# Cross-attention slots in 64 x 64 quarters, with the attended rows copied out of PSUM by VectorE

## The chip, the cores and the metric

The kernel runs on one core of one Trainium2 chip. The metric is the device time of one launch in microseconds (us), of which the median of several runs is taken. TensorE (PE) multiplies, VectorE (DVE), ScalarE (ACT) and GpSimd (POOL) compute element by element, and SyncE (SP) starts most transfers. PEld is TensorE's stream of weight loads.

## The reference

A decoder layer on 16 sequences of 128 tokens with 256 features, in three residual stages: self-attention in emulated fixed point, cross-attention on a context of 128 rows with 128 features, and a feed-forward net with a low-rank part for each of two experts. Only the cross-attention is changed:

```python
qh = (q @ Wq).reshape(B, N, NUM_HEADS, HEAD_DIM).transpose(0, 2, 1, 3)   # 16 heads of 64
kh = (kv @ Wk).reshape(B, M, NUM_HEADS, HEAD_DIM).transpose(0, 2, 1, 3)
vh = (kv @ Wv).reshape(B, M, NUM_HEADS, HEAD_DIM).transpose(0, 2, 1, 3)
attn = jax.nn.softmax(jnp.einsum('bhnd,bhmd->bhnm', qh, kh) * scale, axis=-1)
out = jnp.einsum('bhnm,bhmd->bhnd', attn, vh)
return out.transpose(0, 2, 1, 3).reshape(B, N, INNER) @ Wo + bo
```

## The kernel before

The 16 sequences go in 4 groups (g) of 4, so 512 tokens. The self-attention stage comes first, then the cross-attention stage, then the feed-forward stage. A cross group has 8 **slots** (s), one for each pair of heads. With n = 8 g + s, slot n computes the query, key and value blocks of its pair and its scores, while the softmax, the transposes and the attends lag behind: in slot s TensorE transposes and attends pair n - 3 (`LAG = 3`) and projects pair n - 4. Groups 0 and 1 are written out as straight code and groups 2 and 3 are one loop (`Fori`, L870 for TensorE). Group 1 also merges a low-rank product into feed-forward weights in its slots 3 to 6 (`b_merge`, L783). After the last group come drain slots that finish the lagging work beside the first feed-forward blocks.

TensorE runs its slot in a fixed order, `b_slot` (L792): transposes (L751), q block, v block, projection, k block, attends (L764), scores (L776). Slot 0 splits the projection around transposes, q and v; slot 7 puts the transposes of the next group's normed rows (`normed_T`, L582) between attends and scores. q, k, v and projection go through `split3` (L561 to L566): three products of rounded high and low parts, with full 128 x 128 weights. Attends and scores multiply plain 32-bit floats; an attend has 128 rows (keys) and 64 columns of the array (a head), a score has 64 rows (a head) and 128 columns. The two heads of a pair sit side by side, in the column halves for attends, in the row halves for scores.

PSUM has 8 banks of 128 x 512 floats (L149 to L156): the projection sums in 0 and 1, q and k share bank 2 (`one_ps`), v and the first half of the transposes share bank 3, scores have 4 and 5, the other half of the transposes 6, and the attended rows 7 (`o_ps`).

VectorE's slot (L1392): two reductions of the scores (`neg_max`, L1399), two copies of the transposed weights (`aT_sb`, L1412), the v copy (L1373), parts of the next group's normalisation, the k copy (L1390), the reciprocal (L1445), and the low part of the attended rows (`oT_lo`, L1454). ScalarE's slot (L1062): the q copy (L1096), eight exponentials (L1074), and the high part of the attended rows (`oT_hi`, L1116), read from bank 7. GpSimd scales the exponentials (`b_weights`, L441). Every hand-over is a counting semaphore: `b_S` counts score halves, `b_av` attends, `b_olo` the `oT_lo` that the projection waits for, and so on.

## Time and profile before

| | us |
|---|---|
| median of 3 runs | 642.77 (642.34 to 642.79) |
| the profiled execution | 642.12 |
| its span, first to last instruction | 640.3 |

| engine | busy us | share of the span |
|---|---|---|
| PE | 633.0 | 99% |
| PEld | 548.3 | 86% |
| DVE | 501.2 | 78% |
| ACT | 414.9 | 65% |
| POOL | 346.8 | 54% |

The cross slots run from about 276 us to 522 us of the span. In a row of the timeline stand start, length, engine, line, operation, output and inputs, shape and count; records of one line that follow each other are merged, and the length then goes from the first start to the last end. Each 32-bit product is two records. The end of a matmul record is modelled and lies behind the start of the next one, so rates are read from the distance of starts.

### The profile page before, as it was taken

What the parts mean: (1) busy time and instruction counts of PE and PEld (TensorE: products, weight loads), DVE (VectorE), ACT (ScalarE), POOL (GpSimd) and SP (SyncE); (2) the same over time, 40 slices, a digit from 0 to 9 for tenths busy, and PEclk for the clock granted to TensorE, in tenths of its full rate; (3) what the DMA queues carried; (4) which work ended last, traced back from release to release, by engine and by line L of the source; (5) the groups of instructions that cost most, each with busy time, mean ns of one, the idle gap of its engine ahead of it and who ended that gap; (6) DMA issues with size and microseconds to landing.
All of it is one profiled execution on the core that took longest, in us unless ns stands there. A gap on an engine that the chain in (4) does not pass through costs nothing.

```text
span 640.3 us, 16035 instructions
## 1 busy us (share of the span) xinstructions
PE 633.0 (99%) x5333; PEld 548.3 (86%) x5333; DVE 501.2 (78%) x975; ACT 414.9 (65%) x1458; POOL 346.8 (54%) x742
## 2 busy tenths in 40 slices
PE   8999999999999999999999999999999999999998
PEld 5788888888888888888888888888888888888987
DVE  6888799978998899877777777666667659878765
ACT  4788788888888888887555666565645554434432
POOL 4898376756666666865587675565366433010100
DMA  7954000000000000031100000000000000010010
GB/s 217 383 211 178 1 2 2 2 1 0 0 0 0 0 1 0 16 133 67 48 2 18 1 3 3 16 2 3 1 0 0 0 1 2 1 34 21 12 34 33
DMA packets 10005, 23.14 MB, mean 36 GB/s; under 512 B 1618, under 2 KB 6018, under 8 KB 9058
## 3 DMA queue, kind: packets, MB, share of 16 engines
q1 hardware_dynamic: 7794, 14.63, 6.6%
q0 software_dynamic: 1440, 7.08, 3.1%
q10 hardware_dynamic: 720, 0.79, 0.3%
q8 instruction: 27, 0.44, 0.3%
q14 instruction: 24, 0.20, 0.1%
HBM read 20.40 MB, written 2.10 MB: 35 GB/s over the span
## 4 chain that ended last, share of the span: by engine, by line
PE 92%; POOL 3%; DVE 2%; issue 1%; ACT 1%; DMA 0%; SPq 0%; DVEq 0%; POOLq 0%; ACTq 0%
PE bank L564 21%; PE bank L566 20%; PE bank L565 20%; PE bank L776 5%; PE bank L764 5%; PE bank L751 5%; PE bank L629 5%; PE bank L652 5%; PE bank L618 3%; PE bank L582 2%; PE bank L897 1%; POOL p_int L349 1%; DVE hid L1500 0%; DMA x_sb<-in_x 0%; POOL wv_lo L310 0%
## 5 line engine op out<-in xcount | busy, mean ns | idle before, releaser
L441 POOL TENSOR_SCALAR p_f<-e_sb,rsum 128x128 f32<-128x128 f32 x256 | 90.2, 374 | 83.8 <-DVE rsum L1445 83.4
L349 POOL TENSOR_SCALAR p_int<-e_sb,rsc 128x128 int16<-128x128 f32 x256 | 106.6, 435 | 6.3 <-issue 5.9
L1074 ACT ACTIVATE e_sb<-bank,neg_max 128x128 f32<-128x128 f32 x256 | 90.1, 385 | 4.7 <-DVE neg_max L1399 4.6
L970 ACT ACTIVATE sgn<-bank 128x512 bf16<-128x512 f32 x96 | 54.4, 605 | 33.9 <-PE bank L566 33.9
L985 ACT ACTIVATE e_sb<-si 128x128 f32<-128x128 int16 x256 | 76.1, 314 | 0.2 <-DVE si L1252 0.2
L1230 DVE SCALAR_TENSOR_TENSOR ri<-sgn,bank 128x512 int16<-128x512 bf16 x96 | 63.3, 684 | 12.1 <-ACT sgn L970 10.8
L1096 ACT ACTIVATE q_sb<-bank 128x512 f32<-128x512 f32 x32 | 19.2, 600 | 70.4 <-PE bank L566 70.4
L1074 ACT ACTIVATION_READ_ACCUMULATOR e_sb<-bank,neg_max 128x1 f32 x256 | 57.5, 225 | 0.0
L564 PE MATMUL bank<-xnT_hi,wqk_lo 128*128 128x512 f32 x128 | 53.1, 414 | 1.1 <-DVE ri L1230 0.7
L985 ACT ACTIVATION_READ_ACCUMULATOR e_sb<-si 128x1 f32 x256 | 52.5, 205 | 0.0
L566 PE MATMUL bank<-xnT_hi,wqk_hi 128*128 128x512 f32 x128 | 50.2, 392 | 0.0
L565 PE MATMUL bank<-xnT_lo,wqk_hi 128*128 128x512 f32 x128 | 50.1, 391 | 0.0
L344 POOL TENSOR_TENSOR rsc<-rsum,growth 128x8 f32<-128x8 f32 x32 | 7.4, 232 | 69.8 <-DVE rsum L1286 69.8
L1390 DVE COPY k_sb<-bank 128x512 f32<-128x512 f32 x32 | 22.1, 692 | 27.8 <-PE bank L566 27.7
L1157 ACT CAST oT_hi<-hid 128x512 fp32r<-128x512 f32 x32 | 19.9, 621 | 36.4 <-DVE hid L1500 36.4
L1454 DVE TENSOR_TENSOR oT_lo<-bank,oT_hi 128x512 fp32r<-128x512 f32 x32 | 22.1, 692 | 26.2 <-ACT oT_hi L1116 26.2
L1399 DVE TENSOR_REDUCE neg_max<-bank 128x4 f32<-128x512 f32 x64 | 40.9, 682 | 0.0
L1346 DVE SCALAR_TENSOR_TENSOR si<-s_sgn,bank 128x512 int16<-128x512 bf16 x64 | 40.9, 679 | 0.0
L1412 DVE COPY aT_sb<-bank 128x512 f32<-128x512 f32 x63 | 40.4, 682 | 0.2 <-PE bank L751 0.2
L336 POOL TENSOR_SCALAR veps<-mv 128x4 f32<-128x4 f32 x12 | 3.3, 274 | 64.0 <-DVE mv L1197 63.9
L564 PE MATMUL bank<-wv_hi,xnT_lo 128*128 128x256 f32 x128 | 37.3, 292 | 0.2
L564 PE MATMUL bank<-cw_hi,oT_lo 128*128 128x256 f32 x128 | 36.8, 288 | 0.6 <-DVE oT_lo L1492 0.3
(159 smaller groups left out, 2149.5 us busy)
## 6 DMA issues: line engine op xcount, KB each, us to landing
wB_raw<-in_wB SPq DMA_DIRECT2D x1, 3072.0 KB, 17.6
wB_hi<-in_wB POOLq DMA_DIRECT2D x1, 3072.0 KB, 11.1
wqk_raw<-in_wqk SPq DMA_DIRECT2D x8, 256.0 KB, 8.5
x_sb<-in_x SPq DMA_DIRECT2D x3, 512.0 KB, 16.2
out<-x_sb SPq DMA_DIRECT2D x6, 256.0 KB, 2.2
wqk_hi<-in_wqk POOLq DMA_DIRECT2D x5, 256.0 KB, 7.2
wp_raw<-in_wp SPq DMA_DIRECT2D x1, 1024.0 KB, 13.1
wp_hi<-in_wp POOLq DMA_DIRECT2D x1, 1024.0 KB, 9.1
```

Of the source, the lines that this page charges most:

```text
L349: i = nc.gpsimd.tensor_scalar(p_int[:, half, t, :], e_sb[:, half, t, :], rsc[:, half, t:t + 1], -0.5, ALU.mult, ALU.add)
L441: i = nc.gpsimd.tensor_scalar(p_f[:, half, t, :], e_sb[:, half, t, :], rsum[:, half, t:t + 1], 0.0, ALU.mult, ALU.add)
L564: pe.matmul(out_, wl, mh, start=first, stop=False, **kw)
L565: pe.matmul(out_, wh, ml, start=False, stop=False, **kw)
L566: return pe.matmul(out_, wh, mh, start=False, stop=last, **kw)
L970: nc.scalar.activation(sgn[:, m % 2, :], proj_ps[m % 2][:, :], ACT.Sign).then_inc(a_sgn, 1)
L985: last = nc.scalar.activation(e_sb[:, half, t, :], si[:, i, j * P:(j + 1) * P], ACT.Exp, scale=1.0 / FIX, accum_out=sums[:, t:t + 1])
L1074: last = nc.scalar.activation(e_sb[:, (s - 1) % 2, t, :], s_ps[hh][:, (t % 4) * P:(t % 4 + 1) * P], ACT.Exp, bias=neg_max[:, t:t + 1], sca ...
L1230: V.scalar_tensor_tensor(ri[:, m % 2, :], sgn[:, m % 2, :], -0.5, proj_ps[m % 2][:, :], ALU.mult, ALU.add).then_inc(a_ri, 1)
L1346: V.scalar_tensor_tensor(si[:, i, :], s_sgn[:, i, :], -0.5, s_ps[i][:, :], ALU.mult, ALU.add).then_inc(a_si, 1)
L1399: V.tensor_reduce(neg_max[:, half], s_ps[hh][:, :].rearrange("p (a t) -> p a t", a=GB), AX, ALU.min).then_inc(b_mx, 1)
L1412: V.tensor_copy(aT_sb[:, GB * hh:GB * hh + GB, :].rearrange("p a t -> p (a t)"), pT_ps[hh][:, :]).then_inc((b_pT0, b_pT)[hh], 1)
```

## The change

In the slots from slot 3 of group 0 on (`opens_b` is true for the three before it):

- Scores and attends are issued as 64 x 64 quarters (`b_scores_quarters`, `b_attend_quarters`). Scores: each head's queries are split in two halves. Attends: the keys are split in two halves; the first step takes keys half 0 for two sequences and half 1 for the other two, the second step the opposite, and each adds to one of two banks (`o_pair`).
- TensorE's order becomes transposes, q, k, v, (merge), projection, (next group's transposes), attends step 0, scores, attends step 1.
- Banks: `o_pair` takes half of bank 6 and half of bank 7, which are also k's and q's; v and the two halves of the transposes take 2 and 3.
- VectorE copies the attended rows to a new SBUF tile, `o_raw`, between its two score reductions of the next slot. q waits for that copy (`b_raw`). ScalarE makes `oT_hi` from `o_raw`, and VectorE `oT_lo`, now behind the `aT_sb` copies of the next slot.
- ScalarE does the first four exponentials before the q copy in all slots. VectorE copies k before v. The context's high and low parts for the next group are made in slot 7 in place of slot 0. The loops over groups 2 and 3 are written out for PE, ACT and DVE.
- In the first drain slot the second half of the transposes waits for `b_raw`, and the projection is no longer split.

```diff
--- before.py
+++ after.py
...
+    o_raw, _, nxt = place("o_raw", [P, TOK], F32, at=nxt)
...
-    banks = [nc.alloc_psum_tensor(f"bank{i}", [P, 512], F32) for i in range(8)]
+    banks = [nc.alloc_psum_tensor(f"bank{i}", [P, 512], F32) for i in range(6)]
+    pair = nc.alloc_psum_tensor("pair", [P, 1024], F32)
+    banks += [pair[:, 0:512], pair[:, 512:1024]]
+    o_pair = pair[:, :].rearrange("p (a f) -> p a f", a=2)[:, :, 0:TOK // 2]
     y_ps = banks[0:2]
     proj_ps = banks[2:4]
     s_ps = banks[4:6]
     t_ps = banks[6]
     o_ps = banks[7]
-    one_ps, v_ps = banks[2], banks[3]
-    pT_ps = (banks[3], banks[6])
+    q_ps, k_ps, v_ps = banks[7], banks[6], banks[2]
+    pT_ps = (banks[2], banks[3])
+    first_qk_ps, first_v_ps = banks[2], banks[3]
+    drain_pT_ps = (banks[3], banks[6])
     low_ps = banks[2]
...
             def b_block(g, s, what):
-
+                n = NP * g + s
                 if what == "q":
+                    out_ = first_qk_ps if opens_b(g, s) else q_ps
                     wait(pe, ln_lo, 2 * (G + g) + 2)
-                    wait(pe, b_k, NP * g + s)
+                    if opens_b(g, s):
+                        wait(pe, b_k, n)
+                    else:
+                        wait(pe, b_raw, n - LAG)
+                        if n == LAG:
+                            pe.wait_ge(a_oi, NP * G)
                     for kt in range(KD):
-                        last = split3(one_ps[:, :], [w[kt][:, s * P:(s + 1) * P] for w in (wq_hi, wq_lo)],
+                        last = split3(out_[:, :], [w[kt][:, s * P:(s + 1) * P] for w in (wq_hi, wq_lo)],
                                       [t[:, kt, :] for t in (xnT_hi, xnT_lo)], kt == 0, kt == KD - 1)
...
-                    last = split3(one_ps[:, :], [w[:, s * P:(s + 1) * P] for w in (wk_hi, wk_lo)],
+                    out_ = first_qk_ps if opens_b(g, s) else k_ps
+                    if opens_b(g, s):
+                        wait(pe, b_q, n + 1)
+                    elif n == LAG:
+                        pe.wait_ge(a_aT, NP * G)
+                    if s == 0:
+                        wait(pe, b_clo, g + 1)
+                    last = split3(out_[:, :], [w[:, s * P:(s + 1) * P] for w in (wk_hi, wk_lo)],
...
-                    wait(pe, b_pT0, NP * g + s - LAG + 1)
+                    out_ = first_v_ps if opens_b(g, s) else v_ps
+                    wait(pe, b_pT0, n - LAG + 1)
...
                 last.then_inc(b_blk, 1)
 
-            def b_transpose(n, half, summed=0):
+            def b_transpose(g, s, drain, merging):
+                n = NP * g + s - LAG
+                half = n % 2
                 wait(pe, b_p, n + 1)
-                if isinstance(n, int) and n == 0:
-                    wait(pe, a_aT, NP * G)
-                wait(pe, b_pT, n)
+                if s > 0 and not drain:
+                    wait(pe, b_v, NP * g + s)
+                if n == 0:
+                    pe.wait_ge(b_k, LAG)
                 for hh in range(2):
-                    if hh == 1 and summed:
-                        pe.wait_ge(m_sum, summed)
+                    out_ = (drain_pT_ps if drain else pT_ps)[hh]
+                    if s == 0:
+                        wait(pe, ln_lo, 2 * (G + g) + (2 if drain else hh + 1))
+                    if hh == 0:
+                        wait(pe, b_pT0, n)
+                    else:
+                        wait(pe, b_pT, n)
+                        if drain and s == 0:
+                            wait(pe, b_raw, n)
+                        if merging and s > 3:
+                            pe.wait_ge(m_sum, s - 3)
                     for b in range(GB):
-                        last = pe.transpose(pT_ps[hh][:, b * P:(b + 1) * P], p_f[:, half, GB * hh + b, :], ident[:, :])
+                        last = pe.transpose(out_[:, b * P:(b + 1) * P], p_f[:, half, GB * hh + b, :], ident[:, :])
                 last.then_inc(b_T, 1)
+
+            def b_attend_quarters(n, p, v_count, step):
+
+                if step == 0:
+                    wait(pe, b_pT, n + 1)
+                    wait(pe, b_v, v_count)
+                    wait(pe, b_q, n + LAG + 1)
+                    wait(pe, b_k, n + LAG + 1)
+                else:
+                    wait(pe, b_half, n + 1)
+                for b in range(2):
+                    for keys in range(2):
+                        side = keys ^ step
+                        for hh in range(2):
+                            h0 = (2 * p + hh) * DH
+                            at = slice(keys * DH, (keys + 1) * DH)
+                            last = pe.matmul(o_pair[hh * DH:(hh + 1) * DH, side, b * P:(b + 1) * P],
+                                             v_sb[at, 2 * side + b, h0:h0 + DH], aT_sb[at, GB * hh + 2 * side + b, :],
+                                             start=step == 0 and b == 0, stop=step == 1, skip_group_check=True)
+                last.then_inc((b_half, b_av)[step], 1)
+
+            def b_scores_quarters(n, s):
+                wait(pe, b_q, n + 1)
+                wait(pe, b_k, n + 1)
+                wait(pe, b_e, n)
+                for b in range(GB):
+                    for rows in range(2):
+                        for hh in range(2):
+                            at = b * P + rows * DH
+                            last = pe.matmul(s_ps[hh][rows * DH:(rows + 1) * DH, b * P:(b + 1) * P],
+                                             q_sb[hh * DH:(hh + 1) * DH, s % 2, at:at + DH],
+                                             k_sb[hh * DH:(hh + 1) * DH, s % 2, b * P:(b + 1) * P],
+                                             start=True, stop=True)
+                            if b == GB - 1 and rows == 1:
+                                last.then_inc(b_S, 1)
...
-                    wait(pe, a_oi, NP * G)
+                wait(pe, b_raw, NP * G - LAG)
...
                 if drain:
-                    if s == 0:
-                        project((0, 1))
                     transposes()
                     if s == 0:
                         c_low(0, True)
-                        project((2, 3))
-                    else:
-                        if s < LAG:
-                            c_up(0, s - 1)
-                        project()
+                    elif s < LAG:
+                        c_up(0, s - 1)
+                    project()
...
+                if opens_b(g, s):
...
+                    attend()
+                    b_scores(g, n, s)
+                    return
+                transposes()
+                b_block(g, s, "q")
+                b_block(g, s, "k")
+                b_block(g, s, "v")
+                if merging and s in (3, 4, 5, 6):
+                    wait(pe, b_pT, n - LAG + 1)
+                    b_merge(s - 3)
+                project()
                 if s == NP - 1:
                     def free():
-                        wait(pe, b_k, n + 1)
                         wait(pe, b_v, n + 1)
+                        wait(pe, b_pT, n - LAG + 1)
                     normed_T(G + g + 1, free)
-                b_scores(g, n, s)
+                p = (s - LAG) % NP
+                gg = g if s >= LAG else g - 1
+                v_count = NP * gg + 2 * (p // 2) + 2
+                b_attend_quarters(n - LAG, p, v_count, 0)
+                b_scores_quarters(n, s)
+                b_attend_quarters(n - LAG, p, v_count, 1)
...
-                if first and s == LAG:
-                    act.wait_ge(b_T, 1)
-                    wait(act, a_av, NP * G)
...
                     if first and s < 2:
                         wait(act, a_S, 2 * (NP * G + s) - 2)
-                    nc.scalar.activation(q_sb[:, s % 2, :], one_ps[:, :], ACT.Copy, scale=-DH ** -0.5).then_inc(b_q, 1)
...
+                        act.wait_ge(ld_ctx, 16 * (g + 2))
+                        act.wait_ge(b_blk, BLOCKS * (g + 1))
+                        nc.scalar.copy(cT_hi[:, :], cT_raw[:, :]).then_inc(b_chi, 1)
+                    xnT_high(G + g + 1)
...
-                    nc.scalar.copy(oT_hi[:, :], o_ps[:, :]).then_inc(b_ohi, 1)
-                if s == LAG and not first and not drain:
...
+                        wait(act, b_pj, n - LAG)
+                        nc.scalar.copy(oT_hi[:, :], o_ps[:, :]).then_inc(b_ohi, 1)
+                    else:
+                        wait(act, b_pj, n - LAG)
+                        wait(act, b_raw, n - LAG + 1)
+                        nc.scalar.copy(oT_hi[:, :], o_raw[:, :]).then_inc(b_ohi, 1)
 
             for s in range(NP):
                 b_slot(0, s, first=True)
...
                 n = NP * g + s
@@ -1395,33 +1467,43 @@
                 if (not (first and s == 0)) and not (drain and s >= 1):
                     for hh in range(2):
                         wait(dve, b_S, 2 * n - 1 + hh)
+                        if hh == 1 and n > LAG:
+                            wait(dve, b_av, n - LAG)
+                            wait(dve, b_olo, n - LAG - 1)
+                            V.tensor_copy(o_raw[:, :].rearrange("p (a f) -> p a f", a=2), o_pair).then_inc(b_raw, 1)
                         half = slice(GB * hh, GB * hh + GB)
                         V.tensor_reduce(neg_max[:, half], s_ps[hh][:, :].rearrange("p (a t) -> p a t", a=GB), AX,
...
                     a_out_low(NP * G + s - 1 - LAG)
+                if drain and s == 0:
+                    low_rows(n - LAG - 1, o_raw)
                 if lagged:
                     wait(dve, b_T, n - LAG + 1)
                     if first and s == LAG:
                         wait(dve, a_av, NP * G)
                     wait(dve, b_av, n - LAG)
-                    for hh in range(1 if first and s == LAG else 0, 2):
+                    for hh in range(2):
                         V.tensor_copy(aT_sb[:, GB * hh:GB * hh + GB, :].rearrange("p a t -> p (a t)"),
-                                      pT_ps[hh][:, :]).then_inc((b_pT0, b_pT)[hh], 1)
+                                      (drain_pT_ps if drain else pT_ps)[hh][:, :]).then_inc((b_pT0, b_pT)[hh], 1)
+                if first and s == LAG:
...
+                if opens_b(g, s):
+                    values()
+                    between()
                     b_k_rows(g, s)
+                elif not drain:
+                    b_k_rows(g, s)
...
                     V.reciprocal(rsum[:, (s - 1) % 2, :], sums[:, :]).then_inc(b_rs, 1)
+                if not opens_b(g, s) and not drain:
+                    if merging and s in (3, 4, 5, 6):
+                        merged_sum(s - 3)
...
-                    merged_sum(s - 3)
-                if lagged:
-                    wait(dve, b_ohi, n - LAG + 1)
-                    V.tensor_tensor(oT_lo[:, :], o_ps[:, :], oT_hi[:, :].bitcast(F32), ALU.subtract).then_inc(b_olo, 1)
+                    y_out(G)
+                if drain and lagged:
+                    low_rows(n - LAG, o_ps)
+                if s == NP - 1 and not drain and g < G - 1:
+                    dve.wait_ge(b_chi, g + 2)
...
```

## Rows read from the trace of the kernel before

**Rows 1.** The page, its parts 1 and 4: busy times, and the chain.

```profile
PE 633.0 (99%) x5333; PEld 548.3 (86%) x5333; DVE 501.2 (78%) x975; ACT 414.9 (65%) x1458; POOL 346.8 (54%) x742
...
PE 92%; POOL 3%; DVE 2%; issue 1%; ACT 1%; DMA 0%; SPq 0%; DVEq 0%; POOLq 0%; ACTq 0%
```

**Rows 2.** Windows: stretch, us, busy (records) of PE PEld DVE ACT POOL, clock, DMA.

```profile
303.95:318.71 14.76, 14.76 (x136) 12.76 (x134) 11.16 (x24) 7.96 (x36) 8.23 (x24) 1.00 0.20 52
432.59:447.35 14.76, 14.76 (x136) 12.75 (x134) 10.44 (x20) 7.96 (x36) 8.40 (x20) 1.00 0.01 3
```

**Rows 3.** Timeline of PE, one slot of group 3.

```profile
485.41 1.16 PE L776 MATMUL bank<-k_sb,q_sb 64*128 64x128 f32 x16
486.50 1.09 PE L751 MATMUL bank<-ident,p_f 128*128 128x128 f32 x8
487.35 0.47 PE L564 MATMUL bank<-xnT_hi,wB_lo 128*128 128x512 f32 x1
...
488.82 0.28 PE L564 MATMUL bank<-wB_hi,cT_lo 128*128 128x256 f32 x1
...
489.53 0.28 PE L564 MATMUL bank<-wB_hi,oT_lo 128*128 128x256 f32 x1
...
490.97 0.40 PE L564 MATMUL bank<-cT_hi,wB_lo 128*128 128x512 f32 x1
...
491.44 0.39 PE L566 MATMUL bank<-cT_hi,wB_hi 128*128 128x512 f32 x1
491.76 1.09 PE L764 MATMUL bank<-aT_sb,v_sb 128*64 128x128 f32 x16
```

**Rows 4.** Timeline of PE from later records: second pair, last pair or record.

```profile
484.54 0.93 PE L764 MATMUL bank<-aT_sb,v_sb 128*64 128x128 f32 x14
...
485.20 0.28 PE L764 MATMUL bank<-aT_sb,v_sb 128*64 128x128 f32 x2
...
485.62 0.95 PE L776 MATMUL bank<-k_sb,q_sb 64*128 64x128 f32 x14
...
486.30 0.27 PE L776 MATMUL bank<-k_sb,q_sb 64*128 64x128 f32 x1
```

**Rows 5.** Timeline of DVE in the same slot.

```profile
486.75 1.28 DVE L1399 TENSOR_REDUCE neg_max<-bank 128x4 f32<-128x512 f32 x2
487.94 1.28 DVE L1412 COPY aT_sb<-bank 128x512 f32<-128x512 f32 x2
...
491.87 0.69 DVE L1390 COPY k_sb<-bank 128x512 f32<-128x512 f32 x1 [1.16 <-PE bank L566]
```

**Rows 6.** Timelines of DVE and PEld: a copy, and the weight load that waits for it.

```profile
405.64 1.28 DVE L1412 COPY aT_sb<-bank 128x512 f32<-128x512 f32 x2
...
406.38 0.19 PEld L564 LDWEIGHTS bank<-wB_hi,cT_lo 128*128 128x128 f32 x1 [0.20 <-DVE aT_sb L1412]
```

**Rows 7.** Timeline of PE: scores of slots 3, 4 (group 1), 6, 7, 0, 1.

```profile
364.32 1.16 PE L776 MATMUL bank<-k_sb,q_sb 64*128 64x128 f32 x16
371.94 1.16 PE L776 MATMUL bank<-k_sb,q_sb 64*128 64x128 f32 x16
...
447.35 1.16 PE L776 MATMUL bank<-k_sb,q_sb 64*128 64x128 f32 x16
455.76 1.16 PE L776 MATMUL bank<-k_sb,q_sb 64*128 64x128 f32 x16
463.23 1.16 PE L776 MATMUL bank<-k_sb,q_sb 64*128 64x128 f32 x16
470.65 1.16 PE L776 MATMUL bank<-k_sb,q_sb 64*128 64x128 f32 x16
```

**Rows 8.** Timeline of PE: last scores, the first drain slot's attends.

```profile
515.96 1.16 PE L776 MATMUL bank<-k_sb,q_sb 64*128 64x128 f32 x16
...
520.94 0.77 PE L764 MATMUL bank<-aT_sb,v_sb 128*64 128x128 f32 x10
```

97 lines of the change are left out of this document (41 added, 56 removed).

## The prediction

> **What bounds the kernel now.** I read the page's busy shares and its chain of work first. TensorE is busy 99% of the span and carries 92% of the chain, so only what TensorE issues, or waits for, sets the time [rows 1]. Next I read two windows of two cross slots each, one from the straight-line group 0 and one from the looped group 2: both take 14.76 us, TensorE is busy for all of it at the full granted clock, and VectorE, ScalarE and GpSimd are busy for 10.4 to 11.2, 8.0 and about 8.3 us of it [rows 2]. A slot is 7.38 us with no wait of TensorE, and replacing the loops by straight code costs nothing. Then the timeline of one slot [rows 3], and single records inside it [rows 4], because "busy" hides TensorE's own pauses: a record ends later than the array is free, so only start-to-start distances tell the rate.
>
> Scores (L776) and attends (L764) come as 16 records, two of them side by side in the array. In the attends the last six distances make 485.20 - 484.54 = 0.66, 0.11 a pair; in the scores 486.30 - 485.62 = 0.68, 0.112 a pair [rows 4]. Around them there is dead time. Attends to scores: the last attend pair is through at 485.20 + 0.11 = 485.31, the scores start at 485.41, and their second pair comes 0.21 later in place of 0.11, so this change of form costs 0.10 + 0.10 = 0.20. Key block to attends: 491.44 + 0.24 = 491.68 against 491.76, 0.08, and a first distance of 0.16 (A starts at 484.38, one slot before 491.76), so 0.08 + 0.05. Scores to transposes: 486.30 + 0.11 against 486.50, 0.09 [rows 3, 4].
>
> **What the change takes away.** Scores and attends are now both issued as 64 x 64 quarters, in the order half of the attends (A0), scores (S), other half (A1). Between them the array's form stays the same, so the 0.20 between attends and scores goes (bounds: all of it, or none, rival E). Going in (0.13) and out (0.09 and what follows) stays. The work is the same if four quarters run side by side: A0 and A1 are four steps each and S eight, in place of eight and eight.
>
> **What a step of four costs.** The trace has no step of four. It has two column halves (attends) at 0.11 and two row halves (scores) at 0.112, so 0.11 a step if the two kinds of sharing add up, and 0.22 if only two quarters run at once. Less than 0.11 I exclude, since each record streams as many columns as a record of those rows. I take 0.11, nearest to both rows. The issue speaks for it too: the two records of the last attend pair lie within 485.20 to 485.48 together, one 0.27 long, so they start 0.01 apart or less [rows 4].
>
> **What it adds.** The attended rows now lie in two banks that the next slot's q and k also use. So q(s) has to wait until VectorE has copied them out (o_raw). VectorE does that after its first score reduction. Queued behind the copy on VectorE are the second reduction, both attention copies, oT_lo, the k and v copies and the reciprocal; for q wait TensorE's k, v, projection and all that follows. From the start of the last score record to the start of q's weight load:
> (a) the record lasts 0.27, and VectorE starts 0.04 behind a TensorE record (k block ends at 491.44 + 0.39 = 491.83, its copy starts at 491.87) [rows 3, 5]: 0.31.
> (b) the first reduction: two of them in a row take 487.94 - 486.75 = 1.19 [rows 5]: 0.60.
> (c) the copy, a PSUM to SBUF copy of 128x512 like k's: 0.69 [rows 5].
> (d) VectorE to TensorE's load: attention copy 405.64 + 0.68 = 406.32 (its row of two lasts 1.28, the first takes 0.60), load at 406.38 [rows 6]: 0.05.
> Sum 1.65. Without the wait, A1 takes 0.44 and the way through the transposes is as today: last transpose at 486.50 + 1.09 - 0.27 = 487.32, which is 1.02 behind the last score, and q's load goes with it [rows 3, 4]. That makes 1.46. **So q stands still for 0.19 in each slot, and the 0.20 that was saved is spent again.** A1's end is no limit: 0.44 + 0.31 = 0.75, while the copy cannot start before 0.91.
>
> The rest of the cycle: q 1.50 (487.32 to 488.82), k 0.71 (3 x 0.235, as (491.44 - 490.97) / 2 = 0.235), v 0.71 (489.53 - 488.82), projection 1.44 (490.97 - 489.53), going in 0.08 (above), A0 0.16 + 3 x 0.11 = 0.49, S 7 x 0.112 = 0.79 with the stagger of four records. Together 1.65 + 1.50 + 0.71 + 0.71 + 1.44 + 0.08 + 0.49 + 0.79 = **7.37 against 7.38** [rows 3, 4, 5].
>
> **What else could be late.** VectorE gets one more 0.60 a slot: at most 11.2 + 1.2 = 12.4 of 14.76 [rows 2]. Counted from the last score: copy at 0.91, second reduction 1.51, attention copies 2.11 and 2.71, oT_lo 3.31 to 4.00. The projection's load is due at 1.65 + 1.50 + 0.71 + 0.71 = 4.57, v's (which shares a bank with the first attention copy) at 3.86 against 2.84. k is copied by 4.8 and A0 starts at 6.1. ScalarE starts oT_hi at 1.64 and has then its work of one slot, 7.96 / 2 = 3.98 [rows 2], in front of it, q's copy and the exponentials included: done at 5.6, while the scores, which wait for them, start at 6.6. The reciprocal follows, and feeds GpSimd no later than today. All of these I cost at nothing; their cover is 0.5 to 1.3 us, and should oT_lo lose its 0.57, the projection waits.
>
> **Slots that differ.** 29 slots are in quarters, from slot 3 of group 0.
> - The first has no copy to wait for and its A1 falls behind S: 7.38 - 0.20 - 0.44 = 6.74, -0.64.
> - Slot 7 (four): the eight transposes of the next group now sit between full-array blocks, 8 x 0.11 + 7.37 = 8.25 against 455.76 - 447.35 = 8.41 [rows 7]: -0.16 each, -0.64.
> - Merging slots (four): today 371.94 - 364.32 = 7.62 [rows 7], then 7.37 + 0.235: -0.02 each, -0.08.
> - Slots 0 and 1 of groups 1 to 3: in group 3 they take 463.23 - 455.76 = 7.47 and 470.65 - 463.23 = 7.42 [rows 7], since the projection is split there; I take 0.08 and 0.04 off over the three groups, as group 1's are shorter: -0.24 and -0.12.
> - The other 14: -0.01 each, -0.14.
> - The drain: today 520.94 - (515.96 + 0.89) = 4.09 from the last score to the attends [rows 8]. Then the second half of the transposes needs a bank of o_raw's: 1.65 + 0.44 + low-rank block 1.47 (as many products of the same shape as q, 487.35 to 488.82 [rows 3]) + projection 1.44 + 0.08 = 5.08, of which 0.44 is A1: +0.99.
> Sum: -0.64 - 0.64 - 0.08 - 0.24 - 0.12 - 0.14 + 0.99 = **-0.87 us**. The profiled execution took 642.12 (span 640.3), so it would take 641.25; the median of the runs is 0.65 above that execution, so 641.9.
>
> **Rules of the Trainium skill that speak against it.** In the attends, every record needs weights of its own over all rows, and yet the pairs stay 0.11 apart and TensorE streams without a pause [rows 4]. The Trainium skill ("TensorE: Matmul & The Clock Gate", Part 3, The mechanism) says that a weight load overlaps matmuls in flight only where it goes to another row group. By its price of a load (Part 2, 64 columns at 1.2 per ns, 0.05 us) each step of four would take 0.16, an estimate of +15 us over 28 cycles of 11 distances. This case's rows disagree with the rule, and it gets no chance of its own. The same page (Part 1) puts a floor of about 25 ns between the starts of two matmuls. Four would then just fit a step, but spread over it, which is rival F below; the pairs of this trace, 0.01 apart, disagree.
>
> **Rivals.**
> A, forecast: new wait eats the gain, 641.9. For it: every term of the cycle has a row. Its own range is +-0.08 a cycle, 639.7 to 644.1.
> B, the wait costs nothing (the copy is shorter than k's or the reduction ends earlier): 7.18 a slot, 28 x -0.19 = -5.3, 636.6. Against it: the 0.60 and 0.69 repeat in each slot.
> C, slower: steps of four take 0.125, because four loads and four streams at once share what two did not fill. A0 and S have 11 distances in the cycle, 28 x 11 x 0.015 = +4.6 and 28 x 0.005 for the first, 646.6. It decides from 0.117 a step on (+1.28 us = 0.2%). For it: no row shows four, and the row halves already take a little more (0.112) than the column halves. Against it: those rows bound it closely.
> D, only two quarters at once: 28 x (11 x 0.11 + 4 x 0.11 - 0.19) = +41, 683.
> E, the change doesn't do what it says: moving between quarters of other operands still empties the array, 0.20 stays before S (and A1's is hidden in q's wait): 28 x 0.20 = +5.6, 647.5. Against it: within attends or within scores, other tiles follow each other with no pause [rows 4].
> F, the four records of a step start evenly spread: the last score starts three quarters of a step, 0.08, behind the first of its step and not the 0.02 that I counted; 28 x 0.06 = +1.7, 643.6.
>
> **Chances.** A 0.50, B 0.10, C 0.20, D 0.06, E 0.07, F 0.07. A measurement of this kernel can tell about 0.2% (1.28 us) from no change. The -0.87 of A lies close to -1.28, so of A 0.20 is faster, 0.26 the same, 0.04 slower. F, and 0.05 of C, are the same. Faster 0.30, same 0.38, slower 0.32. The range 639.0 to 647.0 leaves out B and D and some of C's and E's ends.
>
> **What would show it.** In the new trace: a distance of 0.11 between steps of four and none between A0, S and A1 (else C, D, E); q's first load 0.05 behind the end of the o_raw copy, and 0.19 of idle weight loading before it (else B); a distance of 7.37 between the scores of neighbouring slots; slot 7 at 8.25. The forecast is wrong if VectorE's copy isn't what q waits for last, or if the oT_lo, now behind both attention copies, becomes late.

## The result, and the profile after

| | before | after |
|---|---|---|
| median of four runs, us | 642.74 (642.34 to 642.79) | 646.85 (646.81 to 646.99) |
| the profiled execution | 642.12 | 646.87 |
| its span | 640.3 | 645.0 |

The change makes the kernel slower: the ratio is 1.0066, with a 95% interval of 1.0054 to 1.0078, +4.1 us. The forecast was 641.9, -0.87. The time lies inside the range, close to its upper end, but on the other side of no change: the forecast said a little faster.

The page of the changed kernel, its parts 1 and 4 (they answer to [rows 1]):

```profile
PE 634.5 (98%) x6261; PEld 552.3 (86%) x6261; DVE 526.6 (82%) x1005; ACT 412.4 (64%) x1457; POOL 352.3 (55%) x742
...
PE 89%; DVE 5%; POOL 2%; issue 2%; ACT 1%; DVEq 0%; POOLq 0%; ACTq 0%
```

TensorE's busy time grew by 1.5 us only, the span by 4.7; the chain gave 3 of TensorE's 92 points to VectorE. So TensorE now stands still at times. Two windows of two slots each, in the columns of [rows 2]:

```profile
303.99:318.83 14.84, 14.79 (x206) 12.99 (x202) 12.88 (x27) 7.81 (x36) 8.07 (x25) 1.00 0.20 52
435.04:450.31 15.27, 15.03 (x207) 13.04 (x203) 12.39 (x22) 7.81 (x36) 10.02 (x23) 1.00 0.01 2
```

Before, both places took 14.76. Now they differ, and GpSimd is busy for 10.0 us in the slower one. Between the scores of neighbouring slots, from slot 3 of group 0 on, the distances are:

```
group 0:                 7.43 7.41 7.43 8.31
group 1: 7.43 7.41 7.40 7.66 7.66 7.65 9.47 8.31
group 2: 7.47 7.41 7.43 7.75 7.43 7.87 7.40 8.28
group 3: 7.46 7.39 7.42 7.75 7.41 7.88 7.43 8.31
```

There is one 9.47, and four of 7.75 to 7.88; the rest lie 0.02 to 0.06 above the forecast of 7.37, 8.25 and 7.61, and slot 0's of groups 2 and 3 0.09 to 0.10. From slot 2's scores of group 0 to the drain's first attends it is 224.38 us before and 228.47 after: this stretch holds +4.09, all of the difference of the medians. (0.60 more of the span's +4.70 arises ahead of the cross slots, in this one execution.)

One slot, timeline of PE, as [rows 3] and [rows 4] (the last line is from a later record on, the last two steps of the scores):

```profile
503.42 0.67 PE L806 MATMUL pair<-aT_sb,v_sb 64*64 64x128 f32 x16
503.90 1.05 PE L819 MATMUL bank<-k_sb,q_sb 64*64 64x128 f32 x32
504.78 0.62 PE L806 MATMUL pair<-aT_sb,v_sb 64*64 64x128 f32 x16
505.33 1.09 PE L788 MATMUL bank<-ident,p_f 128*128 128x128 f32 x8
506.44 0.47 PE L576 MATMUL pair<-xnT_hi,wB_lo 128*128 128x512 f32 x1
...
511.33 1.05 PE L819 MATMUL bank<-k_sb,q_sb 64*64 64x128 f32 x32
...
504.56 0.40 PE L819 MATMUL bank<-k_sb,q_sb 64*64 64x128 f32 x8
```

The quarters run as forecast: steps at 504.56, 504.67 and then A1 at 504.78, each 0.109 to 0.110 behind the one before, with the four records of a step within 0.02, and no pause between A0, S and A1. VectorE in the same slot (as [rows 5]), and the load that q waits for:

```profile
505.01 0.69 DVE L1475 TENSOR_REDUCE neg_max<-bank 128x4 f32<-128x512 f32 x1 [1.36 <-PE bank L819]
505.62 0.68 DVE L1473 COPY o_raw<-pair 128x512 f32<-128x512 f32 x1
506.21 0.68 DVE L1475 TENSOR_REDUCE neg_max<-bank 128x4 f32<-128x512 f32 x1
506.81 1.28 DVE L1487 COPY aT_sb<-bank 128x512 f32<-128x512 f32 x2
508.01 0.68 DVE L1462 TENSOR_TENSOR oT_lo<-o_raw,oT_hi 128x512 fp32r<-128x512 f32 x1
...
506.41 0.19 PEld L576 LDWEIGHTS pair<-xnT_hi,wB_lo 128*128 128x128 f32 x1 [0.23 <-issue]
```

And the slot of 9.47, timelines of DVE, POOL and PE:

```profile
382.68 1.28 DVE L1487 COPY aT_sb<-bank 128x512 f32<-128x512 f32 x2
383.88 3.20 DVE L1462 TENSOR_TENSOR oT_lo<-o_raw,oT_hi 128x512 fp32r<-128x512 f32 x1
...
383.72 1.43 POOL L475 TENSOR_TENSOR x_sb<-x_sb,raw_b 128x256 f32<-128x256 f32 x2
385.12 1.41 POOL L322 TENSOR_TENSOR cw_lo<-cw_raw,cw_hi 128x256 fp32r<-128x256 f32 x2
...
387.13 0.39 PE L576 MATMUL bank<-wB_hi,oT_lo 128*128 128x256 f32 x1 [1.58 <-DVE oT_lo L1462]
```

The same `oT_lo`, 0.68 at 508.01, takes 3.20 here. It ends 0.55 behind the last of four GpSimd operations, which follow each other without a gap (383.72 + 1.43 = 385.15, the next at 385.12). TensorE's projection stands still for it. The other four long slots look the same with two such GpSimd operations: `oT_lo` takes 1.48, 1.60, 1.49 and 1.61. Not every `oT_lo` that meets GpSimd is held, though. Timelines of POOL and DVE in group 0:

```profile
322.05 1.94 POOL L379 TENSOR_SCALAR raw_b<-zi 128x512 f32<-128x512 int16 x1
...
322.93 0.68 DVE L1462 TENSOR_TENSOR oT_lo<-o_raw,oT_hi 128x512 fp32r<-128x512 f32 x1
```

Here GpSimd reads `zi`, an SBUF tile of 16-bit integers, and `oT_lo` runs inside its record for 0.68 as if alone. The view of waits (engine, what it waited for, sum, times, longest), 300 to 530 us:

```profile
PEld pair L576 <- issue: 6.7, 28, 0.3
...
PEld bank L576 <- DVE oT_lo L1462: 3.3, 5, 1.9
...
PE bank L576 <- DVE oT_lo L1462: 2.0, 3, 1.6
```

**Theories.** P: what changed on VectorE is that `oT_lo` reads two tiles in SBUF (`o_raw`, `oT_hi`) where it read PSUM and SBUF; beside some GpSimd operations it then has to wait, and otherwise a few hundredths a cycle are missing. The slots give the price of the wait: 9.47 against 7.66, and two each of 0.33 and 0.45 over 7.42, together 1.81 + 0.66 + 0.90 = 3.4 us. Rivals: the written-out loops, the order of the work, or the quarters cost it.

### The profile page after: what moved, and what is told of

The parts are those of the page before. It is cut to its first block, busy times and chain, and to the rows that moved or that the text cites. A ratio compares the mean times of both kernels' runs of the same rounds, so it can differ in the third digit from the quotient of the medians.

```text
span 645.0 us, 17840 instructions
## 1 busy us (share of the span) xinstructions
PE 634.5 (98%) x6261; PEld 552.3 (86%) x6261; DVE 526.6 (82%) x1005; ACT 412.4 (64%) x1457; POOL 352.3 (55%) x742
## 4 chain that ended last, share of the span: by engine, by line
PE 89%; DVE 5%; POOL 2%; issue 2%; ACT 1%; DVEq 0%; POOLq 0%; ACTq 0%
PE bank L576 17%; PE bank L577 16%; PE bank L578 16%; PE pair L641 5%; PE bank L664 5%; PE pair L576 4%; PE pair L806 4%; PE bank L788 4%; PE bank L819 4%; PE pair L577 4%; PE pair L578 4%; PE pair L630 3%; PE bank L594 1%; DVE oT_lo L1462 1%; PE pair L583 1%
## 5 line engine op out<-in xcount | busy, mean ns | idle before, releaser
L453 POOL TENSOR_SCALAR p_f<-e_sb,rsum 128x128 f32<-128x128 f32 x256 | 93.4, 385 | 73.6 <-DVE rsum L1532 73.2
L1190 ACT CAST oT_hi<-o_raw 128x512 fp32r<-128x512 f32 x29 | 18.0, 621 | 88.6 <-DVE o_raw L1473 88.6
L1475 DVE TENSOR_REDUCE neg_max<-bank 128x4 f32<-128x512 f32 x64 | 43.6, 686 | 33.3 <-PE bank L819 33.0
L356 POOL TENSOR_TENSOR rsc<-rsum,growth 128x8 f32<-128x8 f32 x32 | 9.5, 297 | 68.3 <-DVE rsum L1354 68.3
L1487 DVE COPY aT_sb<-bank 128x512 f32<-128x512 f32 x61 | 39.1, 680 | 0.0
L576 PE MATMUL bank<-wB_hi,oT_lo 128*128 128x256 f32 x128 | 36.7, 287 | 2.1 <-DVE oT_lo L1462 2.0
L806 PE MATMUL pair<-aT_sb,v_sb 64*64 64x128 f32 x928 | 37.2, 275 | 0.0
```

Source lines behind the costliest of these rows:

```text
L453: i = nc.gpsimd.tensor_scalar(p_f[:, half, t, :], e_sb[:, half, t, :], rsum[:, half, t:t + 1], 0.0, ALU.mult, ALU.add)
L576: pe.matmul(out_, wl, mh, start=first, stop=False, **kw)
L806: last = pe.matmul(o_pair[hh * DH:(hh + 1) * DH, side, b * P:(b + 1) * P], v_sb[at, 2 * side + b, h0:h0 + DH], aT_sb[at, GB * hh + 2 * sid ...
L1475: V.tensor_reduce(neg_max[:, half], s_ps[hh][:, :].rearrange("p (a t) -> p a t", a=GB), AX, ALU.min).then_inc(b_mx, 1)
```

## Experiments

The runs came in five groups; in each the kernel before ran beside them on the same chip, with medians of 642.5 to 643.0.

**GpSimd later.** GpSimd's extra operations wait for `b_olo`, so that they do not meet `oT_lo`; all else is the changed kernel.

```diff
                 if merging and s in (4, 5, 6, 7):
+                    wait(pool, b_olo, NP * g + s - LAG)
                     merged_low(s - 4)
...
+                if not first and (s in (0, 1, 2, 4, 5) if not merging else s in (0, 1, 4, 5)):
+                    wait(pool, b_olo, NP * g + s + 1 - LAG)
```

> The changed kernel, but GpSimd waits for the oT_lo of the slot (b_olo) before its additions to x_sb and its cw_lo subtractions, so that they no longer run beside oT_lo. Theory P (oT_lo now reads two SBUF tiles, o_raw and oT_hi, and is stretched while GpSimd works on SBUF: 3.2 us in one slot, about 1.5 us in four others, in place of 0.68): all oT_lo last 0.68 us, the long slots (9.47, 7.75, 7.87, 7.75, 7.88 us) fall to 7.65 and 7.42, the time falls by 3.4 us to 643.5. Theory Q (oT_lo is late because of its place behind the attention copies or because of what ScalarE hands it): the five long slots stay, 646.9 or more.

Measured 643.74 (643.59 to 643.90), ratio 1.0017 (1.0007 to 1.0027), 3.1 us below the changed kernel. Timelines of DVE, POOL and PEld in the slot that took 9.47:

```profile
384.08 0.68 DVE L1465 TENSOR_TENSOR oT_lo<-o_raw,oT_hi 128x512 fp32r<-128x512 f32 x1
...
378.91 2.26 DVE L1275 TENSOR_SCALAR xn<-x_sb,mv,rstd 128x256 f32<-128x256 f32 x2
381.09 0.67 DVE L1478 TENSOR_REDUCE neg_max<-bank 128x4 f32<-128x512 f32 x1
...
377.83 1.43 POOL L475 TENSOR_TENSOR x_sb<-x_sb,raw_b 128x256 f32<-128x256 f32 x2
379.22 1.42 POOL L322 TENSOR_TENSOR cw_lo<-cw_raw,cw_hi 128x256 fp32r<-128x256 f32 x2
...
382.48 0.19 PEld L579 LDWEIGHTS pair<-xnT_hi,wB_lo 128*128 128x128 f32 x1 [0.78 <-issue]
```

`oT_lo` is back at 0.68, and the slots of 7.75 and 7.88 are at 7.41 to 7.43. This one slot is still at 8.17, for a reason of the same kind at another place: now the two `xn` operations run beside the last three of the four GpSimd operations and take 2.26 (1.15 in the changed kernel), the reduction and the copy behind it are late, and q's load stands 0.78 in place of 0.23. Meeting GpSimd is the cause; where they meet is a matter of order. The kernel before had such a meeting too, timelines of DVE and POOL in slot 5 of group 1, where these `xn` belong:

```profile
376.94 1.75 DVE L1204 TENSOR_SCALAR xn<-x_sb,mv,rstd 128x256 f32<-128x256 f32 x2
...
376.76 1.45 POOL L310 TENSOR_TENSOR cw_lo<-cw_raw,cw_hi 128x256 fp32r<-128x256 f32 x2
```

Two `xn` take 0.68 where no TENSOR_TENSOR of GpSimd runs beside them (at 441.97 in the changed kernel), and 1.75 here, at no cost: the slot takes 7.61, and the other merging slots 7.62 and 7.63.

**ScalarE copies.** The `o_raw` copy goes to ScalarE, first alone and then together with the edit above.

```diff
-                            V.tensor_copy(o_raw[:, :].rearrange("p (a f) -> p a f", a=2), o_pair).then_inc(b_raw, 1)
...
+                        wait(act, b_olo, n - LAG)
+                        nc.scalar.copy(o_raw[:, :].rearrange("p (a f) -> p a f", a=2), o_pair).then_inc(b_raw, 1)
```

> The changed kernel, but ScalarE copies the attended rows to o_raw (before its oT_hi) and VectorE no longer does. Theory W (q waits for the copy, which cannot start on VectorE before the first score reduction is through, and starts 0.09 behind its load after such a wait): the copy starts 0.31 behind the last attend record, 0.75 behind the last score, and ends at 1.34, before q's load is due at 1.46; q's first record moves from 1.75 to 1.49 behind the last score, a slot takes 7.16 in place of 7.42, and 28 slots give 7.3 us: 639.6, if the stretched oT_lo stay as they are. Rival (the copy is not what holds q; the transposes or the quarters themselves do): slots stay at 7.42, 646.9.

> Both edits: ScalarE copies to o_raw, and GpSimd waits for oT_lo. If theories P and W are both right they add, as they touch different slots' waits: 646.9 - 7.3 - 3.4 = 636.2, less some 0.3 more in the first drain slot. If one of them is wrong, its part stays away: 639.6 (P wrong) or 643.5 (W wrong).

Measured 638.42 (638.13 to 639.84), ratio 0.9933 (0.9916 to 0.9949), and with GpSimd later 635.74 (635.64 to 636.06), ratio 0.9894 (0.9877 to 0.9910), 1.1% below the kernel before and 1.7% below the changed kernel. The second one's timelines of PE, ACT and PEld:

```profile
493.32 1.05 PE L822 MATMUL bank<-k_sb,q_sb 64*64 64x128 f32 x32
...
500.48 0.39 PE L822 MATMUL bank<-k_sb,q_sb 64*64 64x128 f32 x6
...
494.88 0.59 ACT L1192 COPY o_raw<-pair 128x512 f32<-128x512 f32 x1 [2.57 <-PE pair L809]
...
495.58 0.19 PEld L579 LDWEIGHTS pair<-xnT_hi,wB_lo 128*128 128x128 f32 x1
```

ScalarE stands idle there and copies at once behind the attends; q's load follows the last transpose with no wait, and the cycle is 500.48 - 493.32 = 7.16. So the wait for VectorE's copy costs 7.42 - 7.16 = 0.26 in each of 28 cycles, 7.3 us. With GpSimd left as it is, six `oT_lo` take 1.25 to 3.31 us in the profiled execution. By the medians 2.7 of the gain is lost again; the profiled execution (639.84, the longest of four) loses 4.1.

**Old forms.** The changed kernel, with scores and attends issued as before (two records side by side, whole rows or columns), in the new order: A0, S, A1.

```diff
-                    for keys in range(2):
-                        side = keys ^ step
-                        for hh in range(2):
...
+                    for hh in range(2):
+                        last = pe.matmul(o_pair[hh * DH:(hh + 1) * DH, step, b * P:(b + 1) * P],
+                                         v_sb[:, 2 * step + b, h0:h0 + DH], aT_sb[:, GB * hh + 2 * step + b, :],
+                                         start=True, stop=True)
```

> The changed kernel, its order, banks, copies and waits, but scores and attends in their old forms (64 x 128 scores, 128 x 64 attends; two sequences' attends before the scores, two behind). Theory D (quarters save the 0.20 between attends and scores; the second change of form, scores to attends, falls into q's wait and costs nothing): slots of 7.62 in place of 7.42, 28 or 29 of them, 646.9 + 5.7 = 652.6. Rival (quarters cost as much as they save): 646.9. Rival (both changes of form count): 646.9 + 11.4 = 658.3.

The same with ScalarE's copy and GpSimd later:

> ScalarE copies, GpSimd waits (the variant at 635.7), but scores and attends in their old forms, half of the attends before and half behind the scores. There is no wait of q left in which a change of form could hide. Theory D (each change of form costs 0.20, the first was seen as 0.25 a slot with the old scores' slower steps): slots of 7.16 + 0.25 + 0.20 = 7.61, 635.7 + 28 x 0.45 = 648.3. Rival (only the change before the scores costs anything): 7.41, 642.7. The difference between the two is what quarters are worth in this order when nothing else waits.

Measured 652.52 (652.04 to 652.61), ratio 1.0154 (1.0137 to 1.0171); and 645.88 (645.75 to 646.37), ratio 1.0053 (1.0036 to 1.0070). PE in the first, and two slots' scores in the second:

```profile
477.24 0.39 PE L803 MATMUL pair<-aT_sb,v_sb 128*64 128x128 f32 x4
477.56 1.16 PE L814 MATMUL bank<-k_sb,q_sb 64*128 64x128 f32 x16
478.65 0.66 PE L803 MATMUL pair<-aT_sb,v_sb 128*64 128x128 f32 x8
...
485.23 1.16 PE L814 MATMUL bank<-k_sb,q_sb 64*128 64x128 f32 x16
```

```profile
495.08 1.16 PE L817 MATMUL bank<-k_sb,q_sb 64*128 64x128 f32 x16
...
502.60 0.60 PE L817 MATMUL bank<-k_sb,q_sb 64*128 64x128 f32 x6
```

With the order of A0, S, A1 the old forms need 7.67 a slot with VectorE's copy and 7.51 with ScalarE's; the quarters need 7.42 and 7.16. So they are worth 0.25 and 0.35 a slot: from A0 to the scores it is 0.488 in place of 0.59, from the scores to A1 0.874 in place of 1.09, as 478.65 - 477.56. The change of form behind S lies inside q's wait, and counts only without it. The second run lies between its two expectations: with the change of form S to A1 the last transpose starts 1.61 behind the last score, with quarters 1.46, so that change costs 0.15 and not 0.20. Some `oT_lo` of the first run are stretched too. One of them, timelines of POOL and DVE:

```profile
339.40 1.88 POOL L385 TENSOR_TENSOR x_sb<-x_sb,raw_b 128x256 f32<-128x256 f32 x2 [0.18 <-POOL raw_b L379]
...
339.46 1.23 DVE L1457 TENSOR_TENSOR oT_lo<-o_raw,oT_hi 128x512 fp32r<-128x512 f32 x1
```

The second `x_sb` starts 0.70 behind the first, as in the slots that are held, so there is no gap; and yet `oT_lo` got in after the first and the second took 1.18 in place of 0.74.

The quarters aren't what made the kernel slower.

**The copy first.** VectorE copies `o_raw` ahead of both reductions, with `oT_lo` between the two `aT_sb` copies and GpSimd later.

> VectorE still copies the attended rows, but before both score reductions, not between them; oT_lo goes between the two attention copies, and GpSimd waits for oT_lo. Theory W (q waits for the end of the copy, whoever makes it): the copy starts 0.75 behind the last score, when the attends are through, ends at 1.44, q's load goes at 1.49 and its first record, 0.09 behind a load that was waited for, at 1.58; slots of 7.25, between 7.42 (copy second) and 7.16 (ScalarE): 635.7 + 28 x 0.09 = 638.2. Rival (VectorE's load is the limit, not the place of the copy): slots stay near 7.42, 643.7.

Measured 639.86 (639.38 to 639.90), ratio 0.9955 (0.9938 to 0.9971). The slots take 7.25 to 7.28 as expected, slot 7 8.15; but the merging ones 7.83, 7.65, 7.64, 7.63, where 7.25 + 0.235 = 7.49 would follow from the expectation. In this order the merge's bank comes free with the last `aT_sb` copy, behind `oT_lo`; the view of waits names that once, with 0.3. Of the 1.7 us above the expectation the four make 0.8 and hundredths in the other slots 0.5; the rest isn't accounted for.

**Written-out loops.** The kernel before with its three loops over groups 2 and 3 written out (`for g in range(2, G)` in place of `Fori`).

> The kernel before, with the loops over groups 2 and 3 of the cross stage written out for TensorE, ScalarE and VectorE as in the change, nothing else. Theory L (loop or straight code costs the same, as groups 0 and 2 take 14.76 us for two slots alike): 642.6, no change. Rival (the longer program costs time by itself): up to some 1 us more.

Measured 642.37 (642.08 to 643.07), ratio 0.9995 (0.9985 to 1.0004): nothing.

**Two SBUF operands in the kernel before.** Only the operands of `oT_lo` change, in its old place in the slot: once it reads two SBUF tiles, and once one, as a copy. Both kernels leave out the low part of the attended rows; they serve for the times alone.

```diff
-                    V.tensor_tensor(oT_lo[:, :], o_ps[:, :], oT_hi[:, :].bitcast(F32), ALU.subtract).then_inc(b_olo, 1)
+                    V.tensor_tensor(oT_lo[:, :], oT_hi[:, :].bitcast(F32), oT_hi[:, :].bitcast(F32), ALU.subtract).then_inc(b_olo, 1)
```

> The kernel before, with one operand changed: VectorE's oT_lo reads oT_hi twice (two SBUF tiles) and not bank 7 and oT_hi, so that the low part of the attended rows is zero (that part of the product is left out). In the kernel before, GpSimd's p_f chain (eight operations, 2.8 us) runs beside each of these oT_lo, which took 0.69 us. Theory P (two SBUF operands make VectorE wait for GpSimd, for the whole chain as in the 3.2 us record of the changed kernel): oT_lo takes some 2.7 us, the reductions start 2.0 us late, slots of about 9.3 us, 642.5 + 29 x 1.95 = 699. If VectorE gets in between two operations of the chain: at most 0.35 more each, 642.5 + 29 x 0.35 = 653 or less. Theory Q (the operands' place is no matter): 642.5 and records of 0.69 us.

> The kernel before, with oT_lo as a plain copy of oT_hi (one SBUF tile read; the low part is wrong by that, its work left out). Theory P with two operands as the condition: 642.5 or less, as one SBUF operand needs no second way in. If an SBUF to SBUF copy on VectorE is itself a double-width form that needs it: records stretched as in the run before, about 699.

Measured 643.47 (643.12 to 643.76), ratio 1.0006 (0.9997 to 1.0016), and 642.87 (642.73 to 643.33), ratio 0.9998 (0.9988 to 1.0008). Timelines of DVE and POOL with two SBUF operands, then POOL at the same place of the slot in the kernel before:

```profile
486.98 0.69 DVE L1454 TENSOR_TENSOR oT_lo<-oT_hi 128x512 fp32r<-128x512 f32 x1 [0.85 <-ACT oT_hi L1116]
...
486.71 1.20 POOL L441 TENSOR_SCALAR p_f<-e_sb,rsum 128x128 f32<-128x128 f32 x2
```

```profile
485.87 1.07 POOL L441 TENSOR_SCALAR p_f<-e_sb,rsum 128x128 f32<-128x128 f32 x3
```

Here `oT_lo` keeps its 0.69, and GpSimd pays: of the two `p_f` operations the second takes 0.85 (three take 1.07 in the kernel before, 0.37 each). The page's group of all 256 `p_f` operations says the same: 90.2 us before, 104.7 with two SBUF operands. So the two engines do exclude each other, but VectorE gets in between two `p_f` operations. GpSimd has time to spare, and the kernel loses nothing that is clear of the noise: three slots of group 1 are 0.61 longer together in this execution. In one of them GpSimd is late, its `raw_b` operation starts 0.24 ahead of VectorE's `cT_lo` (two SBUF inputs), and `cT_lo` takes 0.92 in place of 0.68.

With one SBUF operand, DVE and POOL:

```profile
486.74 0.43 DVE L1454 CAST oT_lo<-oT_hi 128x512 fp32r<-128x512 f32 x1 [0.85 <-ACT oT_hi L1116]
...
486.47 0.93 POOL L441 TENSOR_SCALAR p_f<-e_sb,rsum 128x128 f32<-128x128 f32 x2
```

The copy takes 0.43, and the `p_f` behind it still pays: 0.53 to 0.62 in place of 0.37, 96.6 us for the group. So P was wrong in its condition, since one SBUF operand is enough for a copy, and incomplete: two SBUF operands alone don't hold VectorE for long. In the five long slots of the changed kernel it was a row of TENSOR_TENSORs that held it.

**Gaps.** So the next edit keeps these apart: the second of two waits until the first is through. GpSimd's loop over groups 2 and 3 is written out for it.

```diff
+            def apart(i):
+                gap_at[0] += 1
+                i.then_inc(g_gap, 1)
+                pool.wait_ge(g_gap, gap_at[0])
```

> The changed kernel with one edit: where GpSimd has two TENSOR_TENSORs of two SBUF inputs one behind the other (the two halves of x_sb, of xnT_lo, of cw_lo), the second waits on a semaphore that the first raises when it is through, so that GpSimd stands still for a moment between them. Order, work and banks are those of the changed kernel; GpSimd's loop over groups 2 and 3 is written out for it. Theory P1 (VectorE's oT_lo, which now reads two SBUF tiles, cannot start its data while such GpSimd operations follow each other without a gap, and gets in at the first gap): no oT_lo is longer than the rest of one GpSimd operation and its own 0.68, so about 1.4 us at most; the slot of 9.47 us (group 1, slot 6) comes down by its 1.81 to about 7.7, slots 3 and 5 of groups 2 and 3 from 7.75 and 7.87 to 7.42 to 7.5, and the kernel takes 643.5 to 644.5. Theory P2 (the gap is no matter: VectorE loses to the GpSimd operations by their data rate, or until GpSimd's queue of them is empty): the long oT_lo stay at about 3.2 and 1.5 to 1.6 us, the slots at 9.47, 7.75 and 7.87, and the kernel at 646.9.

Measured 643.76 (643.61 to 644.14), ratio 1.0013 (1.0004 to 1.0023). DVE and POOL in the slot of 9.47:

```profile
383.84 0.75 DVE L1473 TENSOR_TENSOR oT_lo<-o_raw,oT_hi 128x512 fp32r<-128x512 f32 x1
...
384.02 1.98 POOL L484 TENSOR_TENSOR x_sb<-x_sb,raw_b 128x256 f32<-128x256 f32 x2
385.96 1.54 POOL L329 TENSOR_TENSOR cw_lo<-cw_raw,cw_hi 128x256 fp32r<-128x256 f32 x2
```

The slot takes 7.66, the four others 7.41 to 7.43, and the longest `oT_lo` of these slots is 1.07. At 436.96, where GpSimd has begun 0.35 earlier, `oT_lo` takes 0.93 and GpSimd's next one starts 0.08 behind the end of the one before and takes 1.07 in place of 0.73: now it waits. The order of the work is that of the changed kernel, so in these four slots, where GpSimd began 0.21 to 0.36 ahead of `oT_lo` and VectorE got in at the first gap, it is the gap that did it. P1 holds there. In the slot of 9.47 this run shows it less directly: `oT_lo` now starts 0.18 ahead of `x_sb`, and GpSimd waits (its first `x_sb` takes 1.17), where in the changed kernel `x_sb` was ahead by 0.15.

**q's waits.** What was left is 643.76 against a forecast of 641.9, and 7.42 against 7.37 in a cycle. Taken term by term, with S's last record at 504.69, the reduction starts at 0.32, the copy ends at 1.608 (1.60 forecast), q's load comes at 1.724 (1.65), and all behind it fits. The trace has a semaphore instruction of 0.051 between copy and load, on the load's queue: q has two waits. Both runs start from the kernel with gaps. In the first q keeps only `b_raw`; in the second both stay, the other way round.

```diff
-                    wait(pe, ln_lo, 2 * (G + g) + 2)
                     if opens_b(g, s):
+                        wait(pe, ln_lo, 2 * (G + g) + 2)
                         wait(pe, b_k, n)
                     else:
                         wait(pe, b_raw, n - LAG)
+                        wait(pe, ln_lo, 2 * (G + g) + 2)    # only in the second
```

> The kernel with GpSimd's gaps and one edit more: q no longer waits for the normed rows (ln_lo) in the quarter slots, where the transposes of slot 0 have already waited for the same count; so q has one wait left, for the copied rows (b_raw). In the changed kernel's trace the copy ends 1.608 behind the last score's start and q's load starts at 1.724, 0.116 later, where the prediction had 0.05 from a load that carries a single wait; between them stands a semaphore instruction of 0.051 on the load queue. Theory Q (the second wait costs this, because the one that comes last sits in a separate instruction ahead of the load): q's load starts 0.05 behind the copy, slots in quarters shrink by 0.066 from 7.42 to 7.35, 28 of them by 1.85 us in all, so about 641.9 (the kernel with gaps took 643.76, the kernel before 642.6 to 643.0 beside it). Rival R (0.116 is the price of a copy of two banks' halves, or of the load's queue being empty for 0.23): nothing changes, 7.42 and 643.7.

> The kernel with GpSimd's gaps, with q's two waits kept but written the other way round: b_raw first, ln_lo second, so that the wait for the copy is on the load itself and the long-fulfilled one is in the semaphore instruction ahead of it. Theory Q (what costs 0.066 is that the wait that ends last stands in the separate instruction): as with a single wait, 7.35 a slot and 641.9. Rival Q2 (any two waits cost it, in either order): 7.42 and 643.7, though the kernel with one wait gains. Rival R (waits have nothing to do with it): 7.42 and 643.7 in both.

Measured 641.83 (641.62 to 642.13), ratio 0.9987 (0.9977 to 0.9997), and 641.80 (641.52 to 642.27), ratio 0.9985 (0.9976 to 0.9995). The first one's view of waits, its PEld and its scores:

```profile
PEld pair L587 <- DVE o_raw L1484: 4.9, 28, 0.2
```

```profile
501.49 0.19 PEld L587 LDWEIGHTS pair<-xnT_hi,wB_lo 128*128 128x128 f32 x1 [0.17 <-DVE o_raw L1484]
...
499.05 0.40 PE L830 MATMUL bank<-k_sb,q_sb 64*64 64x128 f32 x8
...
506.40 0.29 PE L830 MATMUL bank<-k_sb,q_sb 64*64 64x128 f32 x4
```

The cycle is 506.40 - 499.05 = 7.35, and 28 idle times of the load queue went from 6.7 to 4.9 us. In the second run the load starts 0.055 behind the end of the copy, and its semaphore instruction, for `ln_lo`, is through long before. Two waits in the right order are as good as one: it isn't their number, but whether the one that ends last sits on the load itself or in an instruction ahead of it. Note how the profile names it. In the changed kernel the wait is put down to "issue", a wait for nothing that it shows, since the load itself carried the wait that had long been met; here the same idle time has its name, `o_raw`.

## Why the prediction was wrong

**The step that failed** is in "What else could be late": `oT_lo` was costed at nothing with a cover of 0.57, "and should oT_lo lose its 0.57, the projection waits". It lost it in five slots, for 3.4 us. The time of day was right (3.31 to 4.00 behind the last score; measured 3.32 to 4.00 in most slots), the length wasn't. I took 0.69 from an `oT_lo` that read PSUM and SBUF; the diff shows that it now reads `o_raw` and `oT_hi`, both SBUF. In the kernel before it lay beside GpSimd's `p_f` in every slot and took 0.69, but with other operands and beside another kind of operation; moved behind the `aT_sb` copies it meets `x_sb` and `cw_lo`. Neither question, what is new about its operands and what runs on GpSimd at its new place, was asked. The Trainium skill has the rule ("SBUF — State Buffer", Who interferes with whom): a VectorE instruction with two SBUF inputs contends with a GpSimd instruction that reads SBUF, one waits for the whole of the other, and which one waits depends on who came first. The traces agree in the main. They go further where the wait lasted over up to four GpSimd operations (3.20 us, of which 0.68 is its own). They differ at 322.93, where `oT_lo` took its 0.68 inside a GpSimd operation that reads SBUF; there the measurement decides.

The kernel before could have warned: `xn`, beside `cw_lo` at 376.94, took 1.75 in place of 0.68.

**A term that was mis-sized**: (d), from VectorE's copy to TensorE's load, 0.05 from [rows 6]. Measured 0.116. The load in [rows 6] carries a single wait, q two, with the late one ahead. That is 0.066 in 28 cycles, 1.85 us.

**The sum**: with both taken away the kernel takes 641.83 and 641.80. Its ratio to the kernel before is 0.9987 and 0.9985, -0.81 and -0.84 us; the forecast said -0.87. That it is met so closely is luck in part: the cycle is 7.35 in place of 7.37, and that makes up for the first quarter slot, the drain, and a few slots of 7.39 to 7.45. Term by term:

| term | forecast | after |
|---|---|---|
| step of four | 0.11 | 0.109 |
| pause A0, S, A1 | none | none |
| copy ends behind the last score | 1.60 | 1.608 |
| q's load until A0 | 4.44 | 4.43 |
| A0 + S | 0.49 + 0.79 | 0.488 + 0.784 |
| first quarter slot | 6.74 | 6.82 |
| slot 7 | 8.25 | 8.28 to 8.31 (8.23 to 8.28 with one wait) |
| merging slots | 7.61 | 7.66 (7.59) |
| drain: attends behind the last score | 5.08 | 5.21 |

The drain was sized 0.13 too short and the first quarter slot 0.08; the other terms, beside (d) and what it adds to each slot, lie within 0.02. The drain leg answers to [rows 8]; one line of PE there shows its wait, 0.56 for the copy:

```profile
522.28 0.63 PE L788 MATMUL pair<-ident,p_f 128*128 128x128 f32 x4 [0.56 <-DVE o_raw L1473]
```

**The rivals.** A's mechanism, the new wait takes what the quarters give, is what happened, and ScalarE's copy shows both sides of it: 7.16 a slot without the wait, where B said 7.18. C, D, E and F are wrong: 0.109 a step, four at once, no pause, no spread. C and E carried most of the 0.32 for slower, so the range held the time for the wrong reason. The rule that a weight load overlaps only with another row group (the Trainium skill, "TensorE: Matmul & The Clock Gate", Part 3, The mechanism) would by the prediction's estimate have made each step 0.16; the trace has 0.109 with new weights in all four quarters. The same section also lets a load into the background weight buffer run ahead, which the prediction left out; no run here shows which of the two a load does.

**Open**: when VectorE gets in between two GpSimd operations that follow each other without a gap. Between two `p_f` (TENSOR_SCALAR) operations it did each time. Between two TENSOR_TENSORs of 256 columns it did not in the five long slots, but it did at 339.46 in the run with the old forms, beside the same kind, width and number of inputs, and in the changed kernel at 353.51 (`lb1T`, 32 x 256; `oT_lo` 0.98). So none of the three is the reason, and the runs don't show what is. Open too is why `raw_b` at 322.05 held nobody: `oT_lo` came 0.89 behind its start, while a `cT_lo` that came 0.24 behind the start of another took 0.24 longer, in the kernel before with two SBUF operands.

## What to carry to other kernels

When an edit changes where an operand lives, or moves an operation in its slot, take its duration anew: list its SBUF operands and what GpSimd does at the new place, and check that against its cover. Where an instruction has several waits, see to it that the one that ends last is carried by the instruction itself, and read "issue" ahead of such an instruction as a hidden wait. Where a meeting can't be avoided, a gap between GpSimd's operations can let VectorE in: it took the kernel from 646.9 to 643.8. And a copy that everything waits for belongs on the engine that is idle when its input is ready: the same change with ScalarE's copy and GpSimd out of the way takes 635.7 in place of 646.9.

## What was unexpected of the hardware

- A VectorE TENSOR_TENSOR with two SBUF inputs took 3.20 us in place of 0.68 beside four GpSimd TENSOR_TENSORs without a gap. Beside two of them it took 1.48 to 1.61, and 0.93 to 1.07 when there was a gap between the two. Beside GpSimd's `p_f` TENSOR_SCALARs, reading two SBUF tiles, it took 0.69 to 0.73 in all but two slots (0.82 and 0.86), and the GpSimd operation took 0.80 to 0.88 in place of 0.37. Inside one GpSimd TENSOR_SCALAR of 1.94 us on 16-bit integers (322.05) it took 0.68.
- Two `xn` operations of VectorE, with one SBUF tile of 256 columns as input each, took 2.26 together beside three GpSimd TENSOR_TENSORs, and 0.68 in a slot without them. A copy of one SBUF tile made the GpSimd operation beside it take 0.53 to 0.62 in place of 0.37.
- With the same two waits, a load starts 0.116 or 0.055 behind the end of the copy that it waits for, by their order alone.
- Four quarters of 64 x 64 in 32-bit floats run side by side at 0.109 a step, starting within 0.02 of each other, with new weights each; changing operands between scores and attends costs no time as long as the form stays.
